# The operand halves of the next tiles prepared inside seven weight-product stages, their loads and the last stage's loads reordered, and the first stages' work in another order

## Reference, cut to what matters

```python
q, k, v = x @ Wq, x @ Wk, x @ Wv
attn_out = softmax(q @ k.T * scale) @ v @ Wp + bp            # within each batch of 64 tokens
cms_out = gelu(attn_out @ cW1 + cb1) @ cW2 + cb2 + one_hot(target)
modifier = gelu(concat(attn_out, cms_out) @ mW1 + mb1) @ mW2 + mb2
z = clip(x + cms_out + modifier, 0, 1)
h = gelu(z @ W_down[role] + b_down[role])                    # the adapter, per batch its own role
out = layernorm(z + h @ W_up[role] + b_up[role]) * gamma[role] + beta[role]
```

## Time and profile before

| | us |
|---|---|
| median of 3 runs | 2146.16 (2145.2 to 2148.73) |
| the profiled execution, its own time | 2150.73 |
| its span, first to last instruction | 2149.1 |
| PE busy | 2040.3 (95% of the span) |
| DVE busy | 1437.4 (67%) |
| ACT busy | 968.3 (45%) |
| POOL busy | 76.7 (4%) |

### The profile page before, as it was taken

How to read it: one execution, slowest core, us unless ns; L and a number is a source line. 1 busy time by engine, 2 the same in 40 slices (tenths; PEclk the granted TensorE clock), 3 DMA queues, 4 the chain that set the end, 5 groups by cost and what they waited for, 6 DMA issues and landing times.

```text
span 2149.1 us, 28677 instructions
## 1 busy us (share of the span) xinstructions
PE 2040.3 (95%) x9372; PEld 1681.7 (78%) x9373; DVE 1437.4 (67%) x2701; ACT 968.3 (45%) x1953; POOL 76.7 (4%) x144
## 2 busy tenths in 40 slices
PE   7899999999899999999899999999899999999797
PEld 6778878887778878887678878887678878887676
DVE  6777676555776676556776776556776785554887
ACT  4654443333554443333554453333654453333564
POOL 0000000000000000000000000000000000000122
PEclk9999999999999999999999999999999999999999
DMA  4111131113211132114211231114211222112544
GB/s 168 50 50 59 57 111 59 59 53 134 88 50 58 51 118 59 57 32 157 89 50 44 65 118 59 34 55 157 89 40 50 69 96 64 47 59 104 186 126 114
DMA packets 107966, 171.08 MB, mean 80 GB/s; under 512 B 11645, under 2 KB 71552, under 8 KB 104256
## 3 DMA queue, kind: packets, MB, share of 16 engines
q1 hardware_dynamic: 98672, 126.19, 18.6%
q0 software_dynamic: 9168, 43.26, 6.0%
HBM read 141.62 MB, written 27.79 MB: 79 GB/s over the span
## 4 chain that ended last, share of the span: by engine, by line
PE 84%; DVE 9%; ACT 4%; issue 1%; DMA 1%; SPq 0%; DVEq 0%; POOL 0%; ACTq 0%; POOLq 0%
PE y L1526 17%; PE y L1528 17%; PE y L1527 17%; PE x L1526 10%; PE x L1528 10%; PE x L1527 10%; ACT p_exp L718 1%; DVE s_sb L1199 1%; DVE w_lo L1005 1%; DVE a_forms L1148 1%; PE x L1856 1%; DVE f L1143 1%; DVE t_hi_lo L1238 1%; DMA h_tile<-wp 1%; DVE y_hi_lo L1227 0%
## 5 line engine op out<-in xcount | busy, mean ns | idle before, releaser
L614 ACT CAST w_hi<-w_blocks 128x512 fp32r<-128x512 f32 (+1 forms) x476 | 236.5, 515 | 138.7 <-PE y L1528 85.3
L1005 DVE TENSOR_TENSOR w_lo<-w_blocks,w_hi 128x512 fp32r<-128x512 f32 (+1 forms) x476 | 254.7, 559 | 66.3 <-ACT w_hi L614 66.3
L1526 PE MATMUL x<-h_hi,w_hi 128*128 128x512 f32 x512 | 199.6, 390 | 5.9 <-DVE w_lo L1041 5.9
L1526 PE MATMUL y<-h_hi,w_hi 128*128 128x512 f32 x512 | 199.5, 390 | 5.9 <-DVE w_lo L1041 5.9
L1528 PE MATMUL x<-h_hi,w_lo 128*128 128x512 f32 x512 | 199.3, 389 | 0.0
L1528 PE MATMUL y<-h_hi,w_lo 128*128 128x512 f32 x512 | 199.3, 389 | 0.0
L1527 PE MATMUL x<-h_lo,w_hi 128*128 128x512 f32 x512 | 199.2, 389 | 0.0
L1527 PE MATMUL y<-h_lo,w_hi 128*128 128x512 f32 x512 | 199.2, 389 | 0.0
L1526 PE MATMUL x<-a_forms,w_hi 128*128 128x512 f32 x448 | 178.2, 398 | 18.5 <-ACT f L672 8.3
L1526 PE MATMUL y<-a_forms,w_hi 128*128 128x512 f32 x448 | 174.7, 390 | 6.7 <-DVE f L1099 6.7
L1084 DVE TENSOR_TENSOR h_lo<-f,h_hi 128x512 fp32r<-128x512 f32 x256 | 171.3, 686 | 12.3 <-ACT f L672 11.9
(11 more groups left out here) (239 smaller groups left out, 4230.9 us busy)
## 6 DMA issues: line engine op xcount, KB each, us to landing
w_blocks<-w1m SPq DMA_DIRECT2D x128, 256.0 KB, 3.4
w_blocks<-w1c SPq DMA_DIRECT2D x64, 256.0 KB, 3.2
w_st<-w2c SPq DMA_DIRECT2D x64, 256.0 KB, 3.2
w_st<-w2m SPq DMA_DIRECT2D x64, 256.0 KB, 3.9
zs<-z_by_batch SPq DMA_DIRECT2D x68, 128.0 KB, 2.1
xk_st<-xk POOLq DMA_DIRECT2D x32, 256.0 KB, 3.0
cms<-f SPq DMA_DIRECT2D x32, 256.0 KB, 2.8
z_cms<-cms POOLq DMA_DIRECT2D x8, 1024.0 KB, 6.5
```

Source lines behind the costliest of these rows:

```text
L614: nc.scalar.copy(w1_hi[:, w % RING, cols], src).then_inc(w1_hi_s, 1)
L1005: nc.vector.tensor_tensor(w1_lo[:, w % RING, cols], src, f32(w1_hi[:, w % RING, cols]), ALU.subtract).then_inc(w1_lo_s, 1)
L1526: nc.tensor.matmul(ps, w[0], x[0], start=first, stop=False, skip_group_check=more)
```

## The change

Seven parts.

1. **Passes.** A block of x or xk (128x512, 256 KB) of the next pair is loaded by POOL into `pre_x`, its high half made by ACT (`pre_hi`), its low half by DVE in place, and both are stored to DRAM by POOL. There are 16 to a pair (for s = 0, 1, 2), at three places in each of the seven first mW1 quads: place 0 behind the halves of the second-layer weights, place 1 behind `split_next(Q, 2)`, place 2 behind `split_next(Q, 5)`. The table PRE says how many of these a quad has (the last ones). One block's load waits until the stores of the one before have landed.
2. **Loads.** In the last mW1 quad zr, zc and the halves of the pair's first x tile (2 MB) are loaded behind P2; the second tile's (2 MB) behind P3 and zr and zc. `split_x` and `split_xk` fall away for s > 0. The first pair keeps its own, staged in `h2_tile`.
3. **Tail.** `split_w2(Q, 0)` of a stage's last quad moves ahead of `part`, into the quad.
4. **First quads.** The forms of `a_forms` are numbered anew; P2 and P4 come in halves; `split_q(Q, P3)`, `sum_p6` and `sum_p7` stand ahead of the last forms.
5. **Attention.** `row_max(4)` and its softmax stand ahead of the fourth group's `y`; the softmax on ACT and `inverse` on DVE behind the group before's `y`; `scores(4)` and the second tile's queries earlier on PE; `attended1` of one row block is halved round a `turn_p`. `sort_pairs` moves from ahead of `attention(0)` into it, ahead of `row_max(0)`.
6. **End.** The adapter's up weights come into a tile of their own, `up_st`, after two z loads; their halves stand behind those of z's first block; `down` waits for the first layer's only.
7. **Bias rows.** The b_down rows move from the start to the end.

The diff, cut to its core:

```diff
-RHS = {P1: (0, 2), P2: (1, 3), P3: (4, 8), P5: (5, 9), P7: (6, 10), P6: (7, 11), P4: (12, 13)}
+
+RHS = ({P1: (0, 2), P2: (1, 3), P3: (4, 9), P5: (5, 10), P7: (6, 11), P6: (7, 12), P4: (8, 13)},
+       {P1: (0, 2), P2: (1, 3), P3: (4, 8), P5: (5, 9), P7: (6, 10), P6: (7, 11), P4: (12, 13)})
...
+PRE = (2, 3, 3, 2, 2, 2, 2, 0)
+
+
+def pre_block(Q, place):
+    s, r = divmod(Q, 2 * NQ)
+    q = r - NQ
+    if q < 0 or s == NS - 1 or place < 3 - PRE[q]:
+        return None
+    return 4 * NP * s + sum(PRE[:q]) + place - (3 - PRE[q])
...
+            def pass_x(b):
+
+                s, r = divmod(b, 4 * NP)
+                q, by_token = divmod(r, 2)
+                t, c = 2 * (s + 1) + q // DC, q % DC
+                m = 2 * NP * (s + 1) + q
+                if b:
+                    pool.wait_ge(pre_stored, 32 * b)
+                pool.dma_start(pre_x[:], xk[m] if by_token else xT[t, :, c, :]).then_inc(pre_in, 16)
+                pool.wait_ge(pre_lo_s, b + 1)
+                dst = xk_dram[m] if by_token else x_dram[t, :, :, c, :]
+                pool.dma_start(dst[0], f32(pre_hi[:])).then_inc(pre_stored, 16)
+                pool.dma_start(dst[1], pre_x[:]).then_inc(pre_stored, 16)
...
                 if s + 1 < NS:
-                    load_x(2 * s + 2)
+                    for b in range(4 * NP):
+                        pass_x(4 * NP * s + b)
+                    pool.wait_ge(pre_stored, 32 * 4 * NP * (s + 1))
                 for c in range(DC):
                     pool.wait_ge(c1_stored[c], 16 * (s + 1))
                     pool.wait_ge(c2_stored[c], 16 * (s + 1))
+                pool.wait_ge(prod[P2], 2 * NQ * (s + 1))
                 pool.dma_start(zr[:], xT[2 * s]).then_inc(zr_in, 16)
                 pool.dma_start(zc[:], cf_dram[2 * s]).then_inc(zc_in, 16)
                 if s + 1 < NS:
-                    load_xk(2 * NP * (s + 1))
-                    load_xk(2 * NP * (s + 1) + 1)
-                    load_x(2 * s + 3)
+                    load_x_halves(2 * s + 2)
+                pool.wait_ge(prod[P3], 2 * NQ * (s + 1))
+                pool.wait_ge(zr_in, 16 * (s + 1))
+                pool.wait_ge(zc_in, 16 * (s + 1))
+                if s + 1 < NS:
+                    load_x_halves(2 * s + 3)
+                    load_xk_halves(2 * NP * (s + 1))
+                    load_xk_halves(2 * NP * (s + 1) + 1)
+                else:
...
             sp.wait_ge(prod[P3], 2 * NQ * NS)
-            for n in range(4):
+            for n in range(2):
                 load_z(n, n)
+            sp.dma_start(up_st[:], wu.rearrange("p r k n -> p r (k n)")).then_inc(l1_loaded[1], 16)
+            for n in range(2, 4):
+                load_z(n, n)
...
@@ -1156,11 +1225,11 @@
                 if q:
                     for j in range(2):
                         split_w2(Q - 1, j)
-                if q == 0:
-                    sum_p6(Q)
-                    sum_p7(Q)
+                    split_pre(pre_block(Q, 0))
+                if q:
+                    split_q(Q, P3)
+                else:
                     block22(Q)
-                split_q(Q, P3)
                 if (Q + 1) % NQ or Q // NQ % 2 == 0:
                     weight_sums(Q + 1)
                 if q:
@@ -1173,6 +1242,7 @@
                     block22(Q)
                 split_next(Q, 1)
                 split_next(Q, 2)
+                split_pre(pre_block(Q, 1))
                 block21(Q)
                 hidden_lo(Q, C11)
                 split_next(Q, 3)
@@ -1180,14 +1250,16 @@
                 hidden_lo(Q, C21)
                 split_next(Q, 4)
                 split_next(Q, 5)
+                split_pre(pre_block(Q, 2))
+                if q == NQ - 1:
+                    split_w2(Q, 0)
                 if q:
                     for i in range(3):
                         part(Q - 1, i)
 
             def tail(Q):
                 part(Q - 1, 3)
-                for j in range(2):
-                    split_w2(Q, j)
+                split_w2(Q, 1)
...
                     if s:
                         z1_clip(s - 1, c)
-                split_x(2 * s + 1, DC - 1)
+                if s == 0:
+                    split_x(1, DC - 1)
+                    sort_pairs()
                 if s:
                     z2_sum(s - 1, 0)
                     z2_sum(s - 1, 1)
@@ -1301,17 +1381,16 @@
                     if p == NP:
                         inverse(m + 1)
                     split_pt(m)
-                    if p + 1 < 2 * NP and p not in (NP - 1, NP):
-                        inverse(m + 1)
                     if p and p != NP:
                         split_y(m - 1)
-                    if 0 < p < NP:
-                        query(s, DC + p)
+                    if p == NP - 1:
+                        row_max(m + 1)
+                    if p + 1 < 2 * NP and p != NP:
+                        inverse(m + 1)
+                    if p < NP - 1:
+                        query(s, DC + p + 1)
                     if p in (NP - 1, 2 * NP - 1):
                         split_y(m)
-                    if p == NP - 1:
-                        row_max(m + 1)
-                        inverse(m + 1)
                     if p >= NP:
                         attended1(s, p - NP)
                     if p in (0, 2):
@@ -1332,19 +1411,22 @@
                 difference(g, 7)
                 form(g, 6)
                 split_q(Q, 3)
+                difference(g, 8)
+                form(g, 7)
+                form(g, 8)
                 split_q(Q, 4)
-                form(g, 7)
-                difference(g, 9)
-                form(g, 8)
                 difference(g, 10)
                 form(g, 9)
                 difference(g, 11)
                 form(g, 10)
-                split_q(Q, 5)
                 difference(g, 12)
                 form(g, 11)
+                split_q(Q, 5)
+                form(g, 12)
                 difference(g, 13)
-                form(g, 12)
+                split_q(Q, P3)
+                sum_p6(Q)
+                sum_p7(Q)
                 form(g, 13)
...
             def attention(s):
                 m0 = 2 * NP * s
                 for c in range(DC):
                     query(s, c)
+                    if s == 0 and c == 2:
+                        sort_gather()
+                query(s, DC, (0, 1))
                 scores(m0)
-                query(s, DC)
+                query(s, DC, (2, 3))
                 scores(m0 + 1)
                 for p in range(NP):
                     m = m0 + p
                     turn_p(m)
-                    for c, k in query2_step(p):
-                        query(s, DC + c, (k,))
+                    if p < NP - 1:
+                        query(s, DC + p + 1)
+                    else:
+                        scores(m0 + NP)
                     if p + 2 < NP:
                         scores(m + 2)
                     values(m)
-                scores(m0 + NP)
```

## The result

| | before | changed |
|---|---|---|
| median | 2145.99 (2145.2 to 2148.73, 4 runs) | 2162.6 (2161.88 to 2169.93, 4 runs) |
| the profiled execution, its own time | 2150.73 | 2163.05 |
| its span | 2149.1 | 2161.4 |
| granted clock, mean | 0.989 | 0.979 |

What follows compares the result with a forecast made beforehand. PE, busy for 95% of the span, was taken as the bound. The terms −12 − 4 − 6 − 3.6 + 6 − 0.5 + 21 + 1 gave +1.9 on the median of 2146.16: 2148 us, range 2128 to 2161.

Steps and rivals of the forecast that it cites:

- the main term: First mW1 quads and the quads after: passes chained on one tile hold the second quad, 7.0 us a pair, +21.
- the clock: PE's granted clock: new waits may bring the lower level up to six times, removed ones may spare four; +1 taken.
- P5: +2.0: Second mW1 quad: P5 begins at 793.85 instead of 791.87, since `block12` ends later behind the first pass.
- P4: +4.1 to +5.6: Second mW1 quad: P4 waits for `sum_p7` behind the third block, +4.1; +1.5 more if weight loads slow one load.
- Rival B: Passes' chain: every load and store slowed by weight loads, 5.0 instead of 3.0 us, +4 a pair: 2160; chance 0.18.
- Rival C: Lower clock after each new wait at P4, P5 and the first attention, +1.6 six times: 2157; chance 0.1.
- the cW1 quads' own term: First cW1 quads: sums ahead of the last form let P5 of the second quad begin sooner, −1.5 four times, −6.
- the later three: Attention of pairs 2 to 4: earlier fifth row maximum, −1.2 each, −3.6; saved splits of x and xk off the path.
- The first pair's +5.2: Start and first attention: sort and tile 1's splits ahead of the first scores, +6; bias rows' splits gone, −0.5.
- tails −12: Last quads' tails: both waits of 5.9 us for second-layer weights go, −12, bounds −9 to −12.
- end −4: Adapter at the end: `down` no longer waits for up weights' and z's halves, −4, bounds 0 to −6.
- loads of halves hidden: Last mW1 quad: four 1 MB transfers end by 1008.6, before tile 1's first query at about 1009.8; cost 0.

Runs made afterwards that it cites:

- E10: E5 with P3's weight halves and the sums of P6 and P7 behind the last forms again in the first mW1 quads: 2121.77 us, ratio 0.9895.
- E4: The changed kernel without passes and loads of halves, x and xk loaded and split when the pair begins, as before the change: 2152.7 us, ratio 1.0036.
- E6: E4 with the attention's order from before the change as well: 2127.01 us, ratio 0.9906.
- E3: The changed kernel with the sort back ahead of the first attention: 2165.06 us.
- E5: E1 with the attention's order from before the change for all four pairs, the sort kept at its new place: 2121.88 us, ratio 0.9881.
- E11: The kernel before the change with the tails' edit alone: 2138.3 us, ratio 0.9962.
- E1: The changed kernel with later places for the passes, table (1, 2, 3, 3, 3, 2, 2, 0): 2132.47 us, ratio 0.9938.
- E2: The changed kernel with one 512 KB store for each pass instead of two of 256 KB: 2165.66 us.
- E9: E5 with one 512 KB store for each pass instead of two: 2120.89 us, ratio 0.9889.

## Why the prediction was wrong, step by step

Three steps failed: the main term, 21 us for the second mW1 quads, was too small by 13.5; the clock, at +1 in all, was priced apart from the waits that bring it down; and the end of POOL's program was put at nothing, without a reason.

**The mechanism of the main term was right, its size was not.** The third block at the second quad's place 0 held P4, and the first pass held P5, as forecast. Of the 7.0 us a pair, measured 11.5:

- P5: +2.0 forecast, waits of 2.6.
- P4: +4.1 to +5.6 forecast, waits of 5.5, 5.9 and 7.0. The two turns were forecast at 8.2 each, 16.4 us; they took 18.1, 20.1 and 19.6 in the three pairs. In the second pair the first was 8.35 and the second 11.74: its stores took 3.8 and 5.9 us beside weight loads, its load 3.3. Rival B had this mechanism, with 4 us more for the two turns; 1.7, 3.7 and 3.2 came. The earlier trace rows had shown 5.0 beside such loads, and I had given it 1.5 us for one load. The Trainium skill ("DMA: Bandwidth & Descriptors", "Queues, rings and completion order") says that each DMA engine takes turns packet by packet between the queues that have work; a store of 256 KB with 5.9 us beside two weight loads agrees with that, though the same store took 3.9 and 4.4 us beside two in the other pairs.
- The clock: +1 in all forecast, 8.4 us measured behind these six waits; the lower level followed four of them, all three long ones among them. Rival C had this price (+1.6, six times), and I had set off against it falls that the cW1 quads would be spared. They were spared, all four, but that gain stood in part already in the cW1 quads' own term, and shows there (−7.6). B and C were priced apart, each with the other at nothing, so no case in the range held both.

**A term left out: POOL's end, +4.6.** POOL's program ends, behind its last store, with a DRAIN, and the span ends with it. In the kernel before:

```profile
L79 POOLq DRAIN  x1: 3909/3909/3909, 2145.0 to 2145.0; - x1
```

and in the changed one:

```profile
L95 POOLq DRAIN  x1: 8480/8480/8480, 2152.7 to 2152.7; - x1
```

The change took POOL from 96 transfers to 240.

**Gains left out: the first mW1 quads, −4.7.** I had moved the sums only for what they cost behind them (P5's +2.0), not for P4 of the same quad, which had waited 1.7 us for them. E10 shows the cause.

**Attention: near in sum, wrong in reason.** For the later three −3.6 was forecast, −0.9 measured. I took the splits to be off the path; E4 to E6 show the opposite, 8.5 us in three pairs with the old order and 26.7 with the new one (E4 against the changed kernel). The new order itself costs, and not by waits: in these three attentions PE is idle for 16.5 us instead of 26.4, but its granted clock is 0.93, 0.93 and 0.91 instead of 0.98.

The first pair's +5.2 was forecast (+5.5), and that was luck. The forecast had it from the sort's place and the four splits ahead of the fifth query. The sort's place is refuted (E3, and above all E5). The wait behind the splits is there, 2.6 us, but others have gone: PE is idle for 18.7 us in all up to the end of the first attention, 18.1 before, 18.2 in E5. The difference is the clock. First the kernel before, from the start to the end of the first attention (columns as in the windows above):

```profile
0.00:108.47 108.47, 90.36 (x434) 73.56 (x435) 73.42 (x204) 56.99 (x138) 7.65 (x24) 0.97 0.32 108
```

then the changed kernel, with a part of it:

```profile
0.00:113.67 113.67, 94.92 (x434) 77.33 (x435) 73.53 (x202) 55.65 (x137) 6.37 (x22) 0.92 0.31 103
73.70:84.00 10.30, 8.54 (x29) 7.08 (x29) 7.77 (x26) 3.69 (x14) 1.07 (x2) 0.50 0.40 127
```

and E5:

```profile
0.00:108.10 108.10, 89.85 (x434) 72.88 (x435) 72.64 (x202) 56.22 (x137) 6.37 (x22) 0.98 0.32 108
73.70:84.00 10.30, 8.60 (x53) 7.45 (x53) 7.15 (x25) 5.46 (x17) 0.54 (x1) 1.00 0.33 107
```

In the same 10.3 us PE did 29 matmuls at the lower level and 53 at full clock. The clock had fallen at 73.7 us behind waits of 0.6 and 0.9 us, not behind a long one. In all eight kernels with the new order the first attention has 14 to 24 us at the lower level, in the six with the old one 0 to 7, while the idle time is alike (16.4 to 19.8 and 16.7 to 18.2 us). Which piece of the new order brings the falls was not tried out.

**Right, with sizes:** tails −12 forecast, −14.0 measured in the trace (and E11: only half of it if nothing else makes up for x); first cW1 quads −6, measured −7.6; end −4, measured −5.1, with a wait of 5.0 instead of 8.05 us; loads of halves hidden: no query waits on them.

**The sum.** By the trace the whole is +12.3 against a forecast of +1.9: second quads and their clock +12.9, POOL's end +4.6, later attentions +2.7, first mW1 quads −4.7, the rest −5.0 (tails −2.0, cW1 quads −1.6, end −1.1, first attention −0.3). The medians moved by 16.6, 4.3 us more than the traces. Before's profiled execution lay 4.7 us over its median, as the prediction said, and its nine runs beside E5 go from 2143.48 to 2151.0. In E11's trace, which runs the same code up to the first tail, the start and the first attention are 1.8 us shorter; PE had 3.4 us at the lower clock level there, against 6.8 in before's trace. So at least part of the 4.3 lies in what differs from run to run in the first attention; the rest I cannot place.

## What to carry to other kernels

When work is moved into gaps and passes through one staging tile, compute the chain's turn (issue, stores, landing, load, both splits), and take the landing times of rows that had the same neighbours; then keep places further apart than that turn, counting from when the first load can start. The table of places alone was worth 30 us, 1.4% (E1). A wait on PE costs its length and the slower matmuls behind it, so price the two together. Where two edits are bundled, the gain of one can hide the loss of the other: the attention's new order cost some 10 us (E1 against E5), and in the three later attentions none of it showed, since ready halves paid for it. And an order that shortens PE's waits is not yet faster: look at the granted clock of the same stretch beside the idle time.

## What the runs showed of the hardware that was not expected

POOL's last instruction grows with the transfers that POOL issued: 3.9 and 4.0 us with 96 (before, E4), 7.2 with 192 (E2, E9), 8.5 with 240 (changed, E1, E5). Here the row of E2, with 192:

```profile
L95 POOLq DRAIN  x1: 7176/7176/7176, 2157.7 to 2157.7; - x1
```

That is (8.48 − 3.91) / 144 = 0.032 us for each transfer. It does not go by bytes: E2 moves the same bytes in 48 fewer transfers and took 1.3 us less, 15%, with 3% fewer packets (22224 instead of 22992). It begins behind POOL's last store, so no work hides it.
